# First convolution of a conv / deformable-conv kernel: its in-place chunk is computed ahead of the wait for copied rows, in the place of clock-starting matmuls of zeros

## The chip, the cores and the metric

The kernel runs on one core of one Trainium2 chip. The metric is the device time of one execution in microseconds (us). The engines are PE (TensorE, the matmul array), DVE (VectorE), ACT (ScalarE), POOL (GpSimd) and SP (SyncE, which only issues transfers here). PEld is the loading of PE's weights.

## The reference, cut to what matters

Two blocks work on `x` of shape (4, 32, 64, 64). The change touches the 3x3 convolution at the head of the first.

```python
def _L0_conv_ref(x, ...):        # x is the group-normalized input: one channel a group
    fa = _bn(_conv(x, conv_a_w, conv_a_b, pad=1), ...)      # 16 channels
    fb = _bn(_conv(x, conv_b_w, conv_b_b, pad=1), ...)      # 16 channels
    gh, gw, pr = _position_info(B, H, W, fa.dtype)
    att_a = _bn(_conv(concat([fa, gh, gw]), att_a_w, att_a_b), ...)     # 1x1, to one channel
    map_a = sigmoid(_conv(concat([att_a, gh, gw, pr]), attn_a_w, pad=1))
    ...                                                     # the same for b
    return concat([fa * (map_a * scale1), fb * (map_b * scale2)])

x = x + _L0_conv_ref(_gn(x), ...)
x = x + _L1_conv_ref(_gn(x), ...)    # modulated deformable 3x3 convolution, batch norm, relu
```

So the first convolution is: 4 images, 32 channels in, 32 out (both branches together), 64 x 64 pixels, 9 taps, all in float32.

## The kernel before

A program is written out by hand for each engine, and each engine runs its own instructions in the order in which they stand. Semaphores tie the engines together; a wait holds everything behind it on its engine.

**Where the data is.** The 128 partitions hold 4 images of 32 channels. `x_sb` is the input, `xpad` the normalized input with a border of zeros (image row y is row y + PAD_T). DVE and ACT each write `xpad` in two pieces: NORM1 gives DVE the image rows 0 to 16 and 17 to 33, ACT the rows 34 to 48 and 49 to 63. Each piece adds one to `norm1[0]` (DVE) or `norm1[1]` (ACT); `normalized(pe, norm1, NORM1, rows)` waits until the pieces up to that row are there.

**The first convolution** is done in two steps `s`, each of half the image: SPREAD = 4 chunks `k` of CH_ROWS = 8 rows (512 pixels), one PSUM bank a chunk. A tap of a step is 16 matmuls of 32 x 32 weights over 512 pixels, one for each chunk `k` and image `b`. The matmul of image `b` and chunk `k` takes its rows from the partitions of group (b + k) % 4 and writes those of group b, so that the 16 lie on the 16 different 32 x 32 tiles of the array. For k = 0 the two groups are the same, and the rows are read in place, from `xpad`: these are the 4 tiles of the diagonal. For k = 1, 2, 3 the rows have to stand on other partitions. `turn_rows` copies them there by transfers, six from SP and six from ACT (three a step on each), into `turned[0]` (in the memory of `hy`) and `turned[1]` (in that of `offs`); they count up `turned_in[0]` and `turned_in[1]`. The bank of a chunk gathers the 9 taps of all four images.

**The order on PE** around the change: a wait for the weights; a wait for DVE's first piece of `xpad`; `start_clock(20)`, 20 matmuls of the first padding rows of `xpad`, which are zeros, into the last bank; the waits for the normalized rows and for the copies of step 0; the 9 taps of step 0, after which `conv_ready` lets DVE and ACT move the four banks to `f_sb` (in the memory of `preg`, lines L1262 and L959); the waits for step 1; its taps 0 to 3; `att_step(0)`, 12 matmuls of 128 x 32 weights (L631), which need the moved banks of step 0; the taps 4 to 8 of step 1; then the attention maps of the chunks (`map_chunk`, L642), between which DVE, ACT and POOL put the block's output together and take the statistics of the second block.

Each float32 matmul has two records in the trace, so a tap of 16 matmuls shows as 32. Behind this stage come the offsets of the deformable convolution (L707, also 16 matmuls of 32 x 32 weights over 512 pixels a tap) and its long sampling loop (L844, from about 105 us to 310 us).

Of the kernel before, what the change touches and what calls it, by code (L numbers as in the profile page):

```python
# [7 lines left out]
B, C, H, W = 4, 32, 64, 64  # L8
NPIX = H * W
KK = 9  # L10
BR = C // 2
P128 = B * C
PAD_T = 2
XR, XC = H + 6, W + 2
AR = H + 2
CH_ROWS = 8
# [17 lines left out]
SPREAD = 4  # L34
# [19 lines left out]
BANK = 512  # L54
# [8 lines left out]
def conv_deform_kernel(nc, d, scratch, out):  # L63
# [8 lines left out]
    with ctx:  # L72
        def sb(name, shape, dt=f32):
            return ctx.enter_context(nc.sbuf_tensor(name, shape, dt))

        def sem(name):
            return ctx.enter_context(nc.semaphore(name))
# [3 lines left out]
        xpad = sb("xpad", [P128, XR, XC])  # L81
# [82 lines left out]
        ps = ctx.enter_context(nc.psum_tensor("ps", [P128, 8 * BANK], f32))  # L164
# [27 lines left out]
        norm1 = [sem(f"norm1_{n}") for n in ("vector", "scalar")]  # L192
# [4 lines left out]
        conv_ready = sem("conv_ready")  # L197
# [155 lines left out]
        NORM1 = ((0, 17), (17, 34)), ((34, 49), (49, H))  # L353
# [8 lines left out]
        def made_rows(i):  # L362

            return 2 * (i // B) + ZLEAD + i % B // 2, i % 2 * ZH
# [17 lines left out]
        def normalized(eng, done, pieces, rows):  # L382

            for n, sem_ in enumerate(done):
                needed = sum(pair[n][0] < rows for pair in pieces)
                if needed:
                    eng.wait_ge(sem_, needed)
# [215 lines left out]
        def _(pe):  # L603

            pe.wait_ge(w0_loaded, 16 * SPREAD)

            def conv_taps(s, taps):

                for t in taps:
                    dy, dx = t // 3, t % 3  # L610
                    for k in range(SPREAD):
                        for b in range(B):
                            g = slice((b + k) % SPREAD * C, ((b + k) % SPREAD + 1) * C)
                            if k == 0:
                                r = SPREAD * s * CH_ROWS + PAD_T - 1 + dy
                                rows = xpad[g, r:r + CH_ROWS, dx:dx + W]
                            else:
                                rows = turned[s][g, k, dy:dy + CH_ROWS, dx:dx + W]
                            at = (SPREAD * s + k) * BANK
                            mm = pe.matmul(ps[b * C:(b + 1) * C, at:at + BANK], w0[g, t, :], rows,  # L620
                                           start=t == 0, stop=t == KK - 1,
                                           tile_position=((b + k) % SPREAD * C, b * C))
                return mm
# [19 lines left out]
                          attrep[:, c * CH_ROWS + 1:(c + 1) * CH_ROWS + 1, 0:W],  # L643
                          start=True, stop=True).then_inc(map_ready, 1)

            def start_clock(n):


                for _ in range(n):
                    pe.matmul(ps[0:XC, 7 * BANK:7 * BANK + PAD_T * XC], xpad[:, 0, :], xpad[:, 0:PAD_T, :],  # L650
                              start=True, stop=True)

            pe.wait_ge(norm1[0], 1)
            start_clock(20)
            normalized(pe, norm1, NORM1, SPREAD * CH_ROWS + 1)
            pe.wait_ge(turned_in[0], 16 * len(TURNS))
            conv_taps(0, range(KK)).then_inc(conv_ready, 1)
            normalized(pe, norm1, NORM1, H)
            pe.wait_ge(turned_in[1], 16 * len(TURNS))
            conv_taps(1, range(0, 4))  # L660
            pe.wait_ge(attw_ready, 1)
            pe.wait_ge(fpad_zeroed, 2)
            att_step(0)
            conv_taps(1, range(4, KK)).then_inc(conv_ready, 1)
            pe.wait_ge(mapw_ready, 1)
            pe.wait_ge(pos_loaded, 16 * 2)
# [3 lines left out]
            for c in range(2, NCH):  # L670
# [6 lines left out]
                      start=True, stop=True).then_inc(codes_made, 1)  # L677
# [127 lines left out]
            for i in range(NT // 2):  # L805
# [20 lines left out]
                if 0 <= m < len(FAR_BLOCKS):  # L826
# [4 lines left out]
                              start=True, stop=True).then_inc(first_zmade, 1)  # L831

                if i < MAKERS:
                    n, at = made_rows(i)
# [13 lines left out]
                for turn in range(2):  # L848
# [5 lines left out]
                    elif turn == 1 and i == REACH_TURN + 1:  # L854
                        pe.wait_ge(reach_col, 1)
                        pe.matmul(ps[:, REACH_AT:REACH_AT + P128], later_far[:, :], identf[:, :],
                                  start=True, stop=True)
                    elif turn == 1 and i == REACH_TURN + 2:
                        pe.wait_ge(next_col, 1)
                        pe.matmul(ps[0:1, REACH_AT:REACH_AT + P128], reach_c[:, 1:2], identf[:, :],  # L860
                                  start=True, stop=True)
# [59 lines left out]
        def _(act):  # L921
# [21 lines left out]
            for _, (r0, r1) in NORM1:  # L943
                act.activation(inner[:, r0:r1, :], x3[:, r0:r1, :], ACT.Identity, bias=col(NSH), scale=col(RSTD))\
                    .then_inc(norm1[1], 1)
# [42 lines left out]
            for _, (r0, r1) in NORM2:  # L988
                act.activation(inner[:, r0:r1, :], x3[:, r0:r1, :], ACT.Identity, bias=col(NSH2), scale=col(RSTD2))\
                    .then_inc(norm2[1], 1)  # L990
# [663 lines left out]
```

## Time and profile before

| | |
|---|---|
| median of 3 runs | 334.06 us |
| lowest and highest of them | 333.67 and 336.54 us |
| the profiled execution's own time | 335.25 us |
| its span in the profile | 333.5 us |
| busy over the span | PE 79%, PEld 55%, DVE 81%, ACT 72%, POOL 63% |
| time from 0 to the first taps of the first convolution | 21.3 us |

The time is measured over the whole execution; the span runs from the first to the last profiled instruction. A busy share is an average over stages that differ: in the first 20 us DVE takes statistics and normalizes, from 21 us to 43 us PE computes the first convolution, and the sampling loop fills most of the rest. Times within the profile are counted from the start of the span.

### The profile page before, as it was taken

To read this page: it belongs to the slowest core of one execution; us is meant where nothing else is said; L and a number is where in the kernel's file an instruction comes from. 1 tells how busy PE (TensorE), PEld (TensorE's weight loads), DVE (VectorE), ACT (ScalarE), POOL (GpSimd) and SP (SyncE) were. 2 spreads that over 40 slices of the span, in tenths; PEclk is the share of its full clock that TensorE was granted. 3 is DMA by queue.
4 is the path that set the end of the run, shared out by engine and by line. 5 is a ranking of instruction groups with operands and counts; after the bars stand their busy time and mean duration, and the time that the engine had idled before them with its cause. 6 is when DMAs were issued, how large, how long until landed. Compare 5 with 4: busy or idle time off the path is not lost. (4 is left out here: it accounts for less than half of the span.)

```text
span 333.5 us, 16311 instructions
## 1 busy us (share of the span) xinstructions
PE 264.8 (79%) x7285; PEld 182.7 (55%) x7286; DVE 271.6 (81%) x513; ACT 238.8 (72%) x352; POOL 209.8 (63%) x162
## 2 busy tenths in 40 slices
PE   0399996988957887887899999998989998898340
PEld 0377422432416565656667676667656666776340
DVE  4743378824586999999999999998989999999676
ACT  1321355553865999888799999999989998997016
POOL 9200034400424878898789989998888999898300
PEclk9999997999997999999999999999999999999775
DMA  7891000000240120220000012000000200000006
GB/s 266 159 212 29 2 3 0 15 11 2 50 62 20 37 59 20 93 65 4 4 5 4 4 39 110 4 5 5 4 4 4 110 37 7 3 4 5 4 0 252
DMA packets 11956, 14.35 MB, mean 43 GB/s; under 512 B 4269, under 2 KB 7918, under 8 KB 11848
## 3 DMA queue, kind: packets, MB, share of 16 engines
q1 hardware_dynamic: 9852, 11.34, 11.7%
q10 hardware_dynamic: 1952, 1.34, 2.2%
q8 instruction: 58, 0.95, 1.3%
q0 software_dynamic: 80, 0.61, 0.9%
q14 instruction: 14, 0.11, 0.1%
HBM read 4.73 MB, written 2.98 MB: 23 GB/s over the span
## 5 line engine op out<-in xcount | busy, mean ns | idle before, releaser
L1439 DVE TENSOR_TENSOR prod<-ps,hy 128x480 f32<-128x480 f32 (+1 forms) x256 | 137.9, 600 | 7.6 <-PE ps L844 1.4
L844 PE MATMUL ps<-zreg,hx 64*64 64x96 f32 x4608 | 124.9, 248 | 19.6 <-DVE prod L1439 15.2
L585 POOL TENSOR_TENSOR prod<-prod 128x832 f32<-128x832 f32 x64 | 128.7, 2010 | 17.3 <-DVE prod L1439 15.0
L844 PEld LDWEIGHTS ps<-zreg,hx 64*64 64x64 f32 x4608 | 109.8, 133 | 38.6 <-ACT hx L1104 25.0
L995 ACT ACTIVATE hx<-ps 128x576 f32<-128x576 f32 x129 | 76.9, 648 | 19.2 <-PE ps L725 15.3
L1104 ACT ACTIVATE hx<-hx,rbias 128x1152 f32<-128x1152 f32 x63 | 79.8, 1267 | 0.4
L589 POOL TENSOR_TENSOR prod<-prod 128x320 f32<-128x320 f32 x64 | 50.7, 792 | 5.0
L1447 DVE TENSOR_REDUCE areg<-prod 128x64 f32<-128x576 f32 x64 | 48.3, 755 | 2.6 <-POOL prod L589 0.6
L725 PE MATMUL ps<-wz,xpad 32*64 32x144 f32 (+1 forms) x1024 | 35.1, 322 | 2.9 <-issue 1.3
L1099 ACT ACTIVATE zreg<-ps 128x576 f32<-128x576 f32 x56 | 37.0, 660 | 0.0
L561 POOL TENSOR_TENSOR x_sb<-prod,x_sb 128x512 f32<-128x512 f32 x8 | 10.1, 1268 | 42.4 <-DVE prod L1279 42.1
L693 PE MATMUL ps<-preg,sel 26*128 26x288 bf16 x256 | 26.9, 285 | 7.8 <-DMA preg<-scratch 4.1
L725 PEld LDWEIGHTS ps<-wz,xpad 32*64 32x64 f32 x1024 | 15.5, 130 | 23.3 <-issue 18.0
L707 PE MATMUL ps<-xpad,hx 32*32 32x512 f32 x576 | 20.9, 598 | 0.7 <-DVE zreg L1342 0.6
L620 PE MATMUL ps<-xpad,wreg 32*32 32x512 f32 x144 | 18.5, 595 | 0.4 <-DMA hy<-xpad 0.4
L937 ACT ACTIVATE small<-small 128x1 f32<-128x1 f32 (+1 forms) x5 | 1.0, 203 | 24.4 <-DVE small L1174 19.2
L650 PE MATMUL ps<-xpad 128*66 128x132 f32 x40 | 7.4, 370 | 13.6 <-DVE xpad L1217 13.6
L570 POOL CAST prod<-wreg 128x512 bf16<-128x512 f32 x4 | 3.7, 915 | 22.0 <-DVE wreg L1327 22.0
L1342 DVE COPY zreg<-ps 128x1152 f32<-128x1152 f32 x4 | 5.4, 1358 | 14.4 <-PE ps L725 14.4
L693 PEld LDWEIGHTS ps<-preg,sel 26*128 26x128 bf16 x256 | 7.8, 92 | 17.2 <-issue 5.6
L650 PEld LDWEIGHTS ps<-xpad 128*66 128x66 f32 x40 | 7.2, 201 | 13.2 <-issue 13.2
L707 PEld LDWEIGHTS ps<-xpad,hx 32*32 32x32 f32 x576 | 7.4, 103 | 9.8 <-issue 8.4
(158 smaller groups left out, 265.9 us busy)
## 6 DMA issues: line engine op xcount, KB each, us to landing
zreg<-zreg SPq DMA_DIRECT2D x12, 288.0 KB, 2.4
out<-x_sb SPq DMA_DIRECT2D x7, 256.0 KB, 2.1
x_sb<-in_x SPq DMA_DIRECT2D x3, 512.0 KB, 5.0
preg<-scratch SPq DMA_DIRECT2D x12, 54.0 KB
zreg<-in_pos POOLq DMA_DIRECT2D x1, 528.0 KB, 5.2
x_sb<-in_x SPq DMA_DIRECT2D x2, 256.0 KB, 6.5
scratch<-parts SPq DMA_DIRECT2D x12, 36.0 KB
scratch<-prod SPq DMA_DIRECT2D x10, 36.0 KB
```

Of the source, the lines that this page charges most:

```text
L585: pool.tensor_tensor(slots[:, :, 0:2 * moved], slots[:, :, 0:2 * moved], slots[:, :, 2 * KEPT:6 * KK], ALU.add).then_inc(half_folded, 1)
L589: pool.tensor_tensor(slots[:, :, 0:2 * moved], slots[:, :, 0:2 * moved], slots[:, :, 2 * SUMMED:2 * KEPT], ALU.add).then_inc(folded, 1)
L620: mm = pe.matmul(ps[b * C:(b + 1) * C, at:at + BANK], w0[g, t, :], rows, start=t == 0, stop=t == KK - 1, tile_position=((b + k) % SPREAD * ...
L693: mm = pe.matmul(dist_ps(PAIR_BANKS[u])[:, h, :], sel[u * C:u * C + SELK, b, :], px[u][:, :, y // 2 * W + h * HALF:y // 2 * W + (h + 1) * ...
L707: mm = pe.matmul(ps[j * C:(j + 1) * C, at:at + BANK], woff[b * C:(b + 1) * C, t, :], xpad[b * C:(b + 1) * C, r:r + CH_ROWS, dx:dx + W], st ...
L725: mm = pe.matmul(ps[g * W:(g + 1) * W, b * BANK + at:b * BANK + at + c1 - c0], xpad[b * C:(b + 1) * C, n + g * HH, 1:1 + W], wz[b * C:(b + ...
L844: return pe.matmul(g_ps(g, h)[u * W:(u + 1) * W, k - TAPS[h][0], :, :], hx[s, (t + u) % 4, k, :], z_sb[s, b, at:at + 3, k * C:(k + 1) * C] ...
L995: act.activation(hx[:, t % 4, :, :].rearrange("p k (h x) -> p h k x", h=2), dist_ps(bank).rearrange("p h (k x) -> p h k x", k=KK), ACT.Abs)\
L1099: act.activation(z_sb[:, :, n % ZRING, at:at + ZH], zt_ps(KK * HALF, ZH), ACT.Copy)\
L1104: act.activation(dist[:, slot:slot + 2, :], dist[:, slot:slot + 2, :], ACT.Relu, bias=rbias[:, 0:1], scale=-1.0).then_inc(hx_ready, 2)
L1439: mul = vector.tensor_tensor(pv[:, n0:n1], gv, wv[:, n0:n1], ALU.mult)
L1447: vector.tensor_reduce(here, prod[:, i % 2 * 2:i % 2 * 2 + 2, :] .rearrange("p g (a n e) -> p g a e n", a=C // 2, e=2)[:, :, :, :, 0:SUMME ...
```

## The change

`conv_taps` gets an argument `shifts`, the chunks `k` that it computes. The function `start_clock` and its 20 matmuls of zeros go. In their place, behind the same wait for DVE's first piece, stand the in-place chunk (k = 0) of all 9 taps of step 0 and, behind the wait for all normalized rows, that of the taps 0 to 3 of step 1: 13 x 4 = 52 matmuls. The other three chunks of the same taps, 13 x 12 = 156 matmuls, come behind the waits for the copies. The taps 4 to 8 of step 1 keep all four chunks together. The number of useful matmuls is the same.

```diff
-            def conv_taps(s, taps):
+            def conv_taps(s, taps, shifts=range(SPREAD)):
...
-                    for k in range(SPREAD):
+                    for k in shifts:
...
-            def start_clock(n):
-
-
-                for _ in range(n):
-                    pe.matmul(ps[0:XC, 7 * BANK:7 * BANK + PAD_T * XC], xpad[:, 0, :], xpad[:, 0:PAD_T, :],
-                              start=True, stop=True)
-
             pe.wait_ge(norm1[0], 1)
-            start_clock(20)
-            normalized(pe, norm1, NORM1, SPREAD * CH_ROWS + 1)
+            in_place, copied = range(1), range(1, SPREAD)
+            conv_taps(0, range(KK), in_place)
+            normalized(pe, norm1, NORM1, H)
+            conv_taps(1, range(4), in_place)
             pe.wait_ge(turned_in[0], 16 * len(TURNS))
-            conv_taps(0, range(KK)).then_inc(conv_ready, 1)
-            normalized(pe, norm1, NORM1, H)
+            conv_taps(0, range(KK), copied).then_inc(conv_ready, 1)
             pe.wait_ge(turned_in[1], 16 * len(TURNS))
-            conv_taps(1, range(0, 4))
+            conv_taps(1, range(4), copied)
```

Only PE's program changes. In the rows below, `ps<-xpad,wreg` is a matmul of an in-place chunk (`wreg` holds the weights), `ps<-hy,wreg` one of a copied chunk of step 0, `ps<-offs,wreg` one of step 1; x4 and x12 are numbers of matmuls. PE's program from its first wait, before:

```order
L650 MATMUL ps<-xpad 66x132 [waits norm1_vector,w0_loaded]
L650 MATMUL ps<-xpad 66x132 x19
L620 MATMUL ps<-xpad,wreg 32x512 [waits turned_in0,norm1_scalar,norm1_vector]
L620 MATMUL ps<-xpad,wreg 32x512 x3
L620 MATMUL ps<-hy,wreg 32x512 x12
```

The same place of the changed kernel:

```order
L620 MATMUL ps<-xpad,wreg 32x512 [waits norm1_vector,w0_loaded]
L620 MATMUL ps<-xpad,wreg 32x512 x35
L620 MATMUL ps<-xpad,wreg 32x512 [waits norm1_scalar,norm1_vector]
L620 MATMUL ps<-xpad,wreg 32x512 x15
L620 MATMUL ps<-hy,wreg 32x512 [waits turned_in0]
L620 MATMUL ps<-hy,wreg 32x512 x107
```

The 20 matmuls of zeros are gone, 52 matmuls of the diagonal tiles stand ahead of the wait for `turned_in0`, and behind it come groups of 12 without the 4. Next, PE from the end of step 0 to the attention step, before (the lines left out are three more pairs of x4 and x12):

```order
L620 MATMUL ps<-hy,wreg 32x512 x12
L620 MATMUL ps<-xpad,wreg 32x512 [waits turned_in1,norm1_scalar,norm1_vector]
L620 MATMUL ps<-xpad,wreg 32x512 x3
L620 MATMUL ps<-offs,wreg 32x512 x12
...
L631 MATMUL ps<-preg,attw 32x512 [waits f_ready,fpad_zeroed,attw_ready]
L631 MATMUL ps<-preg,attw 32x512 x11
```

The same place of the changed kernel:

```order
L620 MATMUL ps<-hy,wreg 32x512 x107
L620 MATMUL ps<-offs,wreg 32x512 [waits turned_in1]
L620 MATMUL ps<-offs,wreg 32x512 x47
L631 MATMUL ps<-preg,attw 32x512 [waits f_ready,fpad_zeroed,attw_ready]
L631 MATMUL ps<-preg,attw 32x512 x11
L620 MATMUL ps<-xpad,wreg 32x512 x4
```

Between the end of step 0 and the attention step there were 4 taps of 16 matmuls, and there are now 4 of 12.

## Rows read from the trace of the kernel before

**Rows 1.** Timeline of PE, 8 to 50 us: start, length, what, count.

```profile
13.56 7.38 PE L650 MATMUL ps<-xpad 128*66 128x132 f32 x40 [13.56 <-DVE xpad L1217]
21.32 0.63 PE L620 MATMUL ps<-xpad,wreg 32*32 32x512 f32 x4 [0.38 <-DMA hy<-xpad]
...
30.55 0.63 PE L620 MATMUL ps<-xpad,wreg 32*32 32x512 f32 x4
...
35.43 2.78 PE L631 MATMUL ps<-preg,attw 128*32 128x512 f32 x24
38.14 0.63 PE L620 MATMUL ps<-xpad,wreg 32*32 32x512 f32 x4
...
43.59 1.98 PE L642 MATMUL ps<-zreg,wreg 128*128 128x512 f32 x4
```

**Rows 2.** Waits of PE from 0 to 70 us: total, times, longest.

```profile
PE ps L650 <- DVE xpad L1217: 13.6, 1, 13.6
PE ps L642 <- DVE prod L1279: 2.2, 2, 1.9
PE ps L642 <- DVE zreg L1271: 1.2, 1, 1.2
...
PE ps L620 <- DMA hy<-xpad: 0.4, 1, 0.4
```

**Rows 3.** Timeline of ACT and DVE from 0 to 40 us.

```profile
31.61 1.45 ACT L959 ACTIVATE preg<-ps,small 128x512 f32<-128x512 f32 x2 [8.17 <-PE ps L620]
31.64 1.53 DVE L1262 TENSOR_SCALAR preg<-ps,small 128x512 f32<-128x512 f32 x2 [5.36 <-PE ps L620]
```

**Rows 4.** Windows with L650 alone: stretch, length, busy (records) of PE and PEld, granted clock.

```profile
16.50:17.50 1.00, 1.00 (x6) 1.00 (x5) 1.00 1.12 203
17.50:18.50 1.00, 1.00 (x7) 1.00 (x6) 1.00 1.02 214
...
19.00:19.50 0.50, 0.50 (x6) 0.50 (x5) 1.00 1.06 238
19.50:20.00 0.50, 0.50 (x7) 0.50 (x6) 1.00 1.01 222
20.00:20.50 0.50, 0.50 (x7) 0.50 (x6) 1.00 1.04 275
```

**Rows 5.** Timeline of PEld in the attention step, 35.3 to 38.4 us.

```profile
35.43 0.16 PEld L631 LDWEIGHTS ps<-preg,attw 128*32 128x32 f32 x8 [0.84 <-issue]
35.88 0.13 PEld L631 LDWEIGHTS ps<-preg,attw 128*32 128x32 f32 x4 [0.30 <-issue]
36.31 0.13 PEld L631 LDWEIGHTS ps<-preg,attw 128*32 128x32 f32 x4 [0.30 <-issue]
36.74 0.13 PEld L631 LDWEIGHTS ps<-preg,attw 128*32 128x32 f32 x4 [0.30 <-issue]
```

**Rows 6.** Windows of all engines: PE, PEld, DVE, ACT, POOL, granted clock, DMA share, GB/s.

```profile
24.00:25.00 1.00, 1.00 (x52) 0.69 (x34) 0.86 (x5) 0.00 (x0) 0.00 (x0) 1.00 1.03 122
25.00:26.00 1.00, 1.00 (x50) 0.71 (x34) 0.86 (x5) 0.00 (x0) 0.00 (x0) 1.00 0.35 66
26.00:27.00 1.00, 1.00 (x42) 0.63 (x18) 0.28 (x1) 0.00 (x0) 0.00 (x0) 1.00 0.09 21
...
54.00:55.00 1.00, 1.00 (x2) 0.25 (x2) 0.86 (x3) 0.00 (x0) 1.00 (x2) 0.50 0.00 0
```

**Rows 7.** Timeline of PE, 66 to 106 us: taps of L707, transposes of L718.

```profile
82.34 3.40 PE L707 MATMUL ps<-xpad,hx 32*32 32x512 f32 x96 [0.60 <-DVE zreg L1342]
85.67 1.53 PE L718 MATMUL ps<-identf,areg 128*128 128x128 f32 x12
87.83 0.66 PE L718 MATMUL ps<-identf,areg 128*128 128x128 f32 x4 [0.64 <-ACT areg L1024]
...
101.02 3.60 PE L718 MATMUL ps<-identf,wreg 128*128 128x128 f32 x16
```

## The prediction

> **What bounds the kernel now.** I read the order of work on PE first (its timeline), then PE's waits, then what DVE and ACT wait for. PE does nothing of use until DVE has normalized its first piece: 13.6 us [rows 2]. From 13.56 to 20.94 it runs the 20 matmuls of zeros (40 records), waits 0.38 us for the copied rows, and starts the taps at 21.32 [rows 1]. From there to the maps at 43.59 PE has no wait at all: the next ones are those of L642 [rows 2]. DVE and ACT on the other hand wait for PE there, 5.36 and 8.17 us until step 0 is complete [rows 3]. So between 21.3 and 43.6 us PE is the bound, and every microsecond by which its taps end later is handed to DVE, ACT and POOL, which work on the taps' output. Before 21.3 us the bound is the transfer of the copies, and PE has 7.8 us (13.56 to 21.32) in which it could do something useful. The change fills them. The question is whether what it puts there shortens what comes after by as much as it takes.
>
> **What a tap costs.** The nine taps of step 0 run from 21.32 to 30.55 [rows 1]: 9.23 / 9 = 1.03 us for 16 matmuls, side by side on 16 tiles. From 30.55 to 35.43 there are 4 taps: 4 x 1.03 = 4.10, and 0.78 is left over, which I read as the draining of the last matmuls before the array goes over to weights of 128 rows. Then the attention step, 35.43 to 38.14 [rows 1]: 12 matmuls on 4 tiles, three rounds of 4. Its weights are loaded in groups of 4 at 35.88, 36.31 and 36.74 [rows 5], one each 0.43 us, two records a matmul, so one round of 4 matmuls takes 0.86 us. This is the row on which the forecast rests. A round of 4 costs nearly as much as one of 16 (0.86 against 1.03), because each tile must stream its 512 pixels through, however many tiles run beside it. Splitting a tap of 16 into one of 4 and one of 12 therefore saves very little of the second part, and pays the first almost in full.
>
> **The terms.**
> (a) Removed: 20 matmuls of zeros, 7.38 us, and the 0.38 us wait. Both lay under the transfer, so their removal gives nothing by itself; what counts is that PE is free from 13.56 on.
> (b) The clock. One effect of the matmuls of zeros is to be kept in the sum: up to 18.5 us 6 to 7 of their records fall in a microsecond, and from 19.5 us 7 in half a microsecond [rows 4]. [...] Before the change only zeros were slowed. Now useful matmuls stand there. I take 19.25 as the moment.
> (c) The in-place taps, 9 + 4 = 13 rounds of 4 matmuls. [...] From 13.56 to 19.25, 5.69 / 1.72 = 3.31 rounds; the other 9.69 x 0.86 = 8.33 us. End: 27.58. The upper bound for a round is 1.03, the price of one of 16, which would add 13 x 0.17 = 2.2 us.
> (d) The wait for the copies of step 0 costs nothing: they were in by 21.3 [rows 1], 6.3 us before PE asks. The copies of step 1 are asked for later still; the transfers fade between 25 and 27 us [rows 6]. The wait for all normalized rows stands nine rounds in, past 23 us, when DVE and ACT have long gone on.
> (e) The copied taps, 13 rounds of 12. Not in the trace. Bounds: 0.86 (a round of 4) and 1.03 (of 16); 12 lies between, and I take the middle, 0.95. 13 x 0.95 = 12.35, end 39.93; with the bounds 38.8 and 41.0.
> (f) The drain before the attention step, 0.78, as before: 40.71.
> (g) The attention step waits for the moved banks of step 0. Before, DVE had them at 31.64 + 1.53 = 33.17 [rows 3], 2.3 us ahead of 35.43. Now the copied taps of step 0 end about 27.58 + 8.55 = 36.13, one tap of drain and hand-over later (before: 31.64 - 30.55 = 1.09) the moving starts, at 37.2, and ends at 38.75, 2.0 us ahead of 40.71. Still covered, because the cover shrinks from 4 taps of 16 to 4 of 12, by 0.3 us only.
> Sum: the attention step starts at 40.71 instead of 35.43, **5.3 us later**. Nothing behind it changes in order or work, the five last taps of step 1 included, and no engine has other work with which to catch up, so I carry the 5.3 us to the end. The profiled execution (335.25 us, of which 333.5 are span) would become 340.5; against the median of the runs, 334.06, I forecast 339.3.
>
> What can move that: the moment of (b). If the clock were up at once the sum would be 2.85 us less, if it rose 2 us later, 1.0 more. And the later stretches at half clock, such as 54 to 55 us [rows 6], may fall on other work after a shift: 16 records of the transposes at 101 us took 3.60 us, where 12 and 4 at 85.67 and 87.83 took 1.53 + 0.66 = 2.19 [rows 7]. That is 1.4 us either way. With these and the bounds of (e) the forecast's own range is 336.5 to 342.5; the 2.2 us of (c) can take its end to 343.
>
> [...] All four in-place matmuls of a tap write one bank, from four different groups of rows. In the trace the same happens in each of the four banks, and 16 matmuls still go through in 1.03 us; in the second convolution (L707) each group of rows has a bank to itself, and three taps of 16 take 85.67 - 82.34 = 3.33 us, 1.11 a tap [rows 1, 7]. So sharing a bank costs nothing visible.
>
> [...]
>
> **The rivals.**
> 1. Faster: the records decide, not the streaming. If PE were bound by the number of matmuls that it issues, 1.03 us for 16 would be 0.26 for 4 and 0.77 for 12. The 13 in-place rounds would take 13 x 0.52 = 6.8 us even at half clock and be done at 20.3, ahead of the copies; the copied taps would take 21.32 + 13 x 0.77 + 0.78 = 32.1, 3.3 us earlier than 35.43: 330.8. For it speaks that 16 matmuls take longer than 4 (1.03 against 0.86); against it the attention step, where 4 take 0.86 and not 0.26. The point at which it decides: with p for a round of 4 and q for one of 12, PE is at the attention step at 13.56 + 2.85 + 13 (p + q) + 0.78, and that is 35.43 for p + q = 1.40. The forecast has 1.81, and two rounds can't be under 1.72 as long as 0.86 holds for each. Chance of a gain or of no loss by this: 0.07.
> 2. The clock stays down. The in-place rounds use 4 tiles of 16, and no row shows such a thin round for longer than the attention step's 2.7 us. If it does not count as work enough, all 13 rounds take 1.72: 13.56 + 22.4 = 35.9; if the clock then rises at once, the attention step starts at 35.9 + 12.35 + 0.78 = 49.1, 13.6 us late, and if it takes the 5.7 us that it took before, about 2.9 more: 347.7 to 350.6. Against it: PE would be busy without a gap, and the attention step and the zeros keep or raise the clock. Chance 0.09.
> [...] Chance 0.01.
> 4. Little changes: the clock comes up near 14 us, rounds of 12 cost 0.86, and a stretch at half clock falls away further on: 5.3 - 2.85 - 1.2 - 1.4, about 0. Or the later stages hide some of the delay after all. Chance 0.08.
>
> [...]
>
> **How the numbers follow.** The forecast has 0.75, the rivals 0.07, 0.09, 0.01 and 0.08. One per cent, about what a measurement can tell from no change here, is 3.3 us: 330.7 to 337.4. Faster than that: half of rival 1, 0.04. Within it: the rest of rival 1, rival 4 and the lowest part of the forecast's range (0.04), 0.15. Slower: 0.81. The range runs from 336.4 to 343.0: it holds nearly all of the forecast and a part of rival 4, and leaves out rivals 1 to 3.
>
> **What would show it.** In the timeline of PE: in-place records from 13.6 us at a pace of 1.7 us a round, then of 0.86 from about 19; the first `hy` record at 27.6 with no wait before it (right), or at 21.3 after a wait (rival 1), or after 35 (rival 2, with the clock column or the pace at half). Rounds of 12 between 0.86 and 1.03 us. The attention step near 40.7, without a wait. The same number of us behind it as before. I am wrong if a round of 4 on the diagonal is much cheaper than one in the attention step, if the clock behaves otherwise under thin rounds, or if a later stage absorbs the delay.

## Result and the profile after

The changed kernel took 338.21 us (median of 4 runs, 337.80 to 340.98), the kernel before 334.57 (4 runs). The ratio is 1.0109, 95% interval 1.0071 to 1.0148. A second comparison on one chip (e8 below, 10 runs against 29) gave 1.0056, 1.0030 to 1.0082. Both intervals lie above 1. By the medians the change costs 3.6 us in the first comparison and 2.6 in the second, and the second ratio alone would be 1.9 us; the two profiled executions lie 3.0 us apart (338.29 and 335.25). It is slower, by 0.6 to 1.1%.

The timeline of PE after the change, from the first in-place round to the maps, answers to [rows 1]:

```profile
13.83 12.40 PE L620 MATMUL ps<-xpad,wreg 32*32 32x512 f32 x92 [13.83 <-DVE xpad L1211]
25.66 0.80 PE L620 MATMUL ps<-hy,wreg 32*32 32x512 f32 x8
26.05 0.61 PE L620 MATMUL ps<-xpad,wreg 32*32 32x512 f32 x4
26.12 0.77 PE L620 MATMUL ps<-hy,wreg 32*32 32x512 f32 x9
26.48 0.61 PE L620 MATMUL ps<-xpad,wreg 32*32 32x512 f32 x4
26.66 0.66 PE L620 MATMUL ps<-hy,wreg 32*32 32x512 f32 x4
26.91 0.61 PE L620 MATMUL ps<-xpad,wreg 32*32 32x512 f32 x4
27.09 7.50 PE L620 MATMUL ps<-hy,wreg 32*32 32x512 f32 x186
...
38.37 2.78 PE L631 MATMUL ps<-preg,attw 128*32 128x512 f32 x24
41.09 0.63 PE L620 MATMUL ps<-xpad,wreg 32*32 32x512 f32 x4
...
46.53 1.99 PE L642 MATMUL ps<-zreg,wreg 128*128 128x512 f32 x4
```

The in-place rounds start at 13.83, and PE has no wait until the maps: the 0.38 us for the copies are gone, and the next waits of PE are those of L642, as before. But the attention step (L631) starts at 38.37 instead of 35.43, 2.94 us later, and the maps (L642) at 46.53 instead of 43.59, the same 2.94 us. The first matmuls of the sampling loop follow 2.7 us later (108.78 against 106.09), and the span ends 3.0 us later (336.5 against 333.5). So the delay of this stage is the delay of the whole kernel.

How long a round of 4 takes is best read from its weight loads, one group of 4 for each of a round's two records (timeline of PEld):

```profile
16.36 0.23 PEld L620 LDWEIGHTS ps<-xpad,wreg 32*32 32x32 f32 x4 [0.63 <-issue]
17.21 0.22 PEld L620 LDWEIGHTS ps<-xpad,wreg 32*32 32x32 f32 x4 [0.63 <-issue]
18.07 0.22 PEld L620 LDWEIGHTS ps<-xpad,wreg 32*32 32x32 f32 x4 [0.63 <-issue]
18.75 0.13 PEld L620 LDWEIGHTS ps<-xpad,wreg 32*32 32x32 f32 x4 [0.46 <-issue]
19.18 0.13 PEld L620 LDWEIGHTS ps<-xpad,wreg 32*32 32x32 f32 x4 [0.30 <-issue]
19.61 0.13 PEld L620 LDWEIGHTS ps<-xpad,wreg 32*32 32x32 f32 x4 [0.30 <-issue]
```

Up to 18.07 a group comes each 0.85 us, 1.71 a round; from 18.75 each 0.43, 0.86 a round. The pace doubles near 18.6, under rounds that use 4 tiles of 16, and I read it as the clock going from half to full. The clock column says 1.00 from 13 us on, as in [rows 4], and up to 18.6 the pace contradicts it; e7 below has a stretch where the column itself says 0.50 and the weight loads come at half their rate. The second half, the rounds of 12, in windows (engines as in [rows 6]):

```profile
19.00:27.00 8.00, 8.00 (x101) 2.83 (x97) 5.17 (x27) 1.89 (x4) 0.00 (x0) 1.00 0.86 178
27.00:38.00 11.00, 11.00 (x303) 7.88 (x287) 1.53 (x2) 1.45 (x2) 0.00 (x0) 1.00 0.05 14
```

287 weight loads in 11.0 us are 26.1 in a microsecond; a round of 12 has 24, so it takes about 0.9 us, start and end of the stretch included (e6 below shows nine of them in 7.72 us, 0.86 each). DVE takes over step 0 at 35.16, and not at 31.64 as before (second row of [rows 3]):

```profile
35.16 1.53 DVE L1256 TENSOR_SCALAR preg<-ps,small 128x512 f32<-128x512 f32 x2 [8.29 <-PE ps L620]
```

It is done at 36.69, 1.7 us ahead of the attention step, which still does not wait for it.

### The profile page after: what moved, and what is told of

Read it like the earlier page. It is cut to its first block and busy times, and to the rows that moved or that the text cites. A ratio compares the mean times of both kernels' runs of the same rounds, so it can differ in the third digit from the quotient of the medians.

```text
span 336.5 us, 16230 instructions
## 1 busy us (share of the span) xinstructions
PE 265.9 (79%) x7245; PEld 176.8 (53%) x7246; DVE 271.5 (81%) x513; ACT 238.7 (71%) x352; POOL 209.8 (62%) x162
## 5 line engine op out<-in xcount | busy, mean ns | idle before, releaser
L838 PE MATMUL ps<-zreg,hx 64*64 64x96 f32 x4608 | 121.8, 247 | 19.1 <-DVE prod L1433 12.8
L838 PEld LDWEIGHTS ps<-zreg,hx 64*64 64x64 f32 x4608 | 107.9, 132 | 36.9 <-ACT hx L1098 24.3
L701 PE MATMUL ps<-xpad,hx 32*32 32x512 f32 x576 | 20.9, 598 | 0.7 <-DVE zreg L1336 0.6
L620 PEld LDWEIGHTS ps<-xpad,wreg 32*32 32x32 f32 x144 | 6.0, 115 | 24.6 <-issue 23.5
L642 PE MATMUL ps<-zreg,wreg 128*128 128x512 f32 x16 | 9.9, 727 | 3.6 <-DVE prod L1273 2.2
```

What stands on the lines that cost most here:

```text
L701: mm = pe.matmul(ps[j * C:(j + 1) * C, at:at + BANK], woff[b * C:(b + 1) * C, t, :], xpad[b * C:(b + 1) * C, r:r + CH_ROWS, dx:dx + W], st ...
L838: return pe.matmul(g_ps(g, h)[u * W:(u + 1) * W, k - TAPS[h][0], :, :], hx[s, (t + u) % 4, k, :], z_sb[s, b, at:at + 3, k * C:(k + 1) * C] ...
```

## Experiments

Line numbers shift by some lines between the kernels; the names are the same. "Start of the attention step" is the first record of `ps<-preg,attw`, 35.43 in the kernel before and 38.37 after the change.

**e1: in place only the nine rounds of step 0.**

```diff
-            normalized(pe, norm1, NORM1, H)
-            conv_taps(1, range(4), in_place)
+            normalized(pe, norm1, NORM1, SPREAD * CH_ROWS + 1)
             pe.wait_ge(turned_in[0], 16 * len(TURNS))
             conv_taps(0, range(KK), copied).then_inc(conv_ready, 1)
+            normalized(pe, norm1, NORM1, H)
             pe.wait_ge(turned_in[1], 16 * len(TURNS))
-            conv_taps(1, range(4), copied)
+            conv_taps(1, range(0, 4))
```

> In place and early are only the nine rounds of step 0; the taps 0 to 3 of step 1 are whole again (16 matmuls). Theory F (streaming floor): a round of 4 and a round of 12 each cost 0.86 us, a whole tap 1.03 to 1.07, so each split tap costs 0.7 us more than a whole one, and only what lies before 21.3 us is free. Nine rounds, the first 4.7 us of them at half clock, end near 23.9; the attention step should start at 35.6 to 35.8, against 38.37 after the change and 35.43 before it: 0.2 to 0.4 us slower than before, no change that can be measured. Theory C (the loss of the change is only useful work done at half clock): the same cold rounds stand here, so the loss should stay near 3 us. Theory W (the loss is the later hand-over of step 0 to DVE and ACT): the hand-over is still later than before by under 1 us, so the loss is that.

Measured: ratio to before 1.0009 (0.9983 to 1.0036), medians 336.10 and 335.15, no change. Its profile:

```profile
13.35 8.12 PE L620 MATMUL ps<-xpad,wreg 32*32 32x512 f32 x60 [13.35 <-DVE xpad L1211]
21.01 0.69 PE L620 MATMUL ps<-hy,wreg 32*32 32x512 f32 x8
...
34.27 2.78 PE L631 MATMUL ps<-preg,attw 128*32 128x512 f32 x24
```

The loss of the change is gone with the four rounds of step 1, though the first rounds are still at half clock. That speaks against theory C, less strongly than planned: by the weight loads (0.86 us apart up to 15.89, 0.43 from 16.57) the clock was up by 16.4 in this execution, 3.0 us after the first round. For that reason, and with a start at 13.35, the attention step comes even 1.2 us earlier than before, which I had not worked out (35.6 to 35.8); the span (334.2 against 333.5) and the 10 runs show no gain from that. What becomes of such a gain is taken up under e6.

**e2: in place only six rounds.** As e1, with `conv_taps(0, range(6), in_place)`, then `conv_taps(0, range(6), copied)` and `conv_taps(0, range(6, KK))`.

> In place and early are six rounds of step 0, as many as I work out to end at 21.3 us, when the copies are there; taps 6 to 8 and all of step 1 are whole. Theory F: no round lies beyond the free time, and six groups of 12 cost 0.86 instead of 1.03: the attention step starts at 34.4, 1.0 us earlier than before; the ratio to before is 0.997, a gain at the limit of what can be measured. Theory C: the rounds at half clock are under the transfer and cost nothing, no change. If splitting a tap has a price of its own (a drain between the parts), 0 to 1 us slower.

Measured: 0.9980 (0.9957 to 1.0003), medians 334.83 and 335.15. The sign is that of theory F (0.997), but the interval holds 1 as well, which is theory C here, so this run does not decide between them. The profile of this kernel was taken at a mean clock of 0.749, and its times are not read. A loss of more than 0.1 us, the upper end of the interval, is excluded.

**e3: the matmuls of zeros taken away, nothing in their place.**

```diff
             pe.wait_ge(norm1[0], 1)
-            start_clock(20)
             normalized(pe, norm1, NORM1, SPREAD * CH_ROWS + 1)
```

> The kernel before without its 20 matmuls of zeros, nothing put in their place. It measures what the zeros are worth. If the clock starts to rise only when PE starts its taps at 21.3 us, about 5 us of whole taps run at half clock, 1.71 instead of 1.03 us each: 2 us slower than before (1.3 to 2.8). If the clock were up without them, no change.

Measured: 1.0054 (1.0023 to 1.0086), 1.7 us by the medians (336.81 and 335.15). The windows of its profile:

```profile
23.00:25.00 2.00, 2.00 (x50) 1.01 (x35) 1.72 (x9) 0.63 (x2) 0.00 (x0) 1.00 0.79 123
25.00:27.00 2.00, 2.00 (x50) 1.14 (x36) 1.29 (x6) 0.00 (x0) 0.00 (x0) 1.00 0.34 85
27.00:29.00 2.00, 2.00 (x81) 1.42 (x64) 0.00 (x0) 0.00 (x0) 0.00 (x0) 1.00 0.10 23
29.00:31.00 2.00, 2.00 (x85) 1.75 (x68) 0.00 (x0) 0.00 (x0) 0.00 (x0) 1.00 0.00 0
```

35 or 36 weight loads in two microseconds up to 27, 64 to 68 behind: by this pace the first 6 us of whole taps ran at half clock (the column says 1.00 here too), and the attention step starts at 37.89, 2.46 us later than before. So the zeros were worth about 2 us (1.7 by the medians, 2.46 at the attention step), and the in-place rounds, under which the clock rises too (near 18.6 in the profile after the change), replace them in this.

**e4: the changed kernel with the clock raised early.** `start_clock` is defined and called ahead of everything on PE, where the border of `xpad` has just been zeroed (the definition is left out here).

```diff
+            pe.wait_ge(xpad_zeroed, 1)
+            start_clock(24)
             pe.wait_ge(w0_loaded, 16 * SPREAD)
```

> The changed kernel with 24 matmuls of zeros put ahead of all, from the moment the border of the normalized input is zeroed (4.8 us), so that the clock is up when the first useful round starts at 13.8 us. Theory F: 13 rounds at 0.86 end at 25.0, 2.3 us earlier than after the change; the attention step starts at 36.0, still 0.6 us later than before: 2.3 us faster than the changed kernel, 0.6 slower than before. Theory C: the whole loss of 2.9 us goes. If the clock falls again between the zeros and 13.8 us, nothing is gained.

Measured: 0.9982 (0.9954 to 1.0010) to before, medians 335.15 and 335.15: the loss is gone. The changed kernel was not run beside it; set against e8, on another chip, the two ratios to before lie 0.0074 apart, 2.5 us.

```profile
4.79 8.16 PE L609 MATMUL ps<-xpad 128*66 128x132 f32 x48 [4.79 <-POOL xpad L547]
13.48 10.08 PE L629 MATMUL ps<-xpad,wreg 32*32 32x512 f32 x92 [0.53 <-DVE xpad L1220]
22.97 0.80 PE L629 MATMUL ps<-hy,wreg 32*32 32x512 f32 x8
...
35.67 2.78 PE L640 MATMUL ps<-preg,attw 128*32 128x512 f32 x24
```

The attention step starts 2.7 us earlier than after the change and 0.24 later than before; F had 36.0. The clock is up for the useful rounds: 11 records of the zeros fall in the two microseconds up to 10, 19 in the two behind, and the weight loads of the in-place rounds come 0.43 us apart from 13.91 on. By time alone C fits as well here (all but 0.24 of its 2.9 us are gone). e1 and e5 decide between the two.

**e5: the zeros kept where they were, and the in-place rounds behind them.** Now almost nothing of the 13 rounds is hidden and all of them run at full clock. The definition of `start_clock` is kept too and left out here.

```diff
             pe.wait_ge(norm1[0], 1)
+            start_clock(20)
             in_place, copied = range(1), range(1, SPREAD)
             conv_taps(0, range(KK), in_place)
```

> The changed kernel with the 20 matmuls of zeros kept ahead of the in-place rounds, so that these start near 20.9 us, at full clock, and no part of them is hidden by the transfer. It measures the price of splitting 13 taps. Theory F (streaming floor, 0.86 for a round of 4 and of 12): 13 x (0.86 + 0.86) less the 0.9 us by which the two groups overlap where they meet; the attention step starts at 43.1, 7.7 us later than before. If the number of matmuls issued decided, splitting would be free: 13 x 1.03 and the start 0.4 us earlier, no change against before.

Measured: 1.0167 (1.0132 to 1.0203), 341.68 against 335.60 (4 and 29 runs).

```profile
13.64 6.50 PE L650 MATMUL ps<-xpad 128*66 128x132 f32 x40 [13.64 <-DVE xpad L1219]
20.07 10.07 PE L620 MATMUL ps<-xpad,wreg 32*32 32x512 f32 x92
29.56 0.81 PE L620 MATMUL ps<-hy,wreg 32*32 32x512 f32 x8
29.97 0.60 PE L620 MATMUL ps<-xpad,wreg 32*32 32x512 f32 x4
...
42.29 2.78 PE L631 MATMUL ps<-preg,attw 128*32 128x512 f32 x24
```

From the first in-place record to the attention step 22.22 us pass, where 13 whole taps took 14.11 (21.32 to 35.43). Worked out, 13 x 1.72 + 0.78 less an overlap of 0.9 is 22.24. There is no half clock in this stretch (the weight loads come 0.43 us apart from 20.52 on), so theory C cannot explain it, and a bound by the number of matmuls would give 14. The split costs 8.1 us for 13 taps. The attention step comes 6.86 us later than before, and not 7.7, because the rounds start at 20.07 here and not at 20.9: 1.25 us before the whole taps did. The changed kernel sets the 7.5 us from 13.83 to 21.3 against the 8.1, but the first 4.8 of them count half, because of the clock: 8.1 - 7.5 + 2.4 = 3.0, where 2.94 were measured.

**e6: the early zeros of e4 and the nine rounds of e1.** Only as many rounds as fit before the copies.

> The zeros early (24, from 4.8 us), and in place and early only the nine rounds of step 0, which at full clock just fit before the copies: 13.6 + 9 x 0.86 = 21.3. Theory F: nine groups of 12 at 0.86, then nine whole taps: the attention step starts at 34.0, 1.4 us earlier than before, ratio to before 0.996. What comes behind may take from it what the place of the half-clock stretch near 100 us costs (it was 3.4 us long before the change and 10.2 us in two experiments, where the transposes and the first samples took about 1 us more): so 333.2 to 334.6 against 334.6 of before.

Measured: 0.9955 (0.9926 to 0.9985), 334.49 against 335.60 (12 and 29 runs): faster than the kernel before, and 3.7 us faster than the changed one beside it (338.16).

```profile
13.44 7.93 PE L629 MATMUL ps<-xpad,wreg 32*32 32x512 f32 x72 [0.41 <-DVE xpad L1220]
21.58 7.93 PE L629 MATMUL ps<-hy,wreg 32*32 32x512 f32 x209 [0.20 <-DMA hy<-xpad]
...
29.30 0.59 PE L629 MATMUL ps<-offs,wreg 32*32 32x512 f32 x1
...
33.95 2.78 PE L640 MATMUL ps<-preg,attw 128*32 128x512 f32 x24
```

The rounds end 0.20 us before the copies land, which is the fit aimed at. The nine copied rounds run from 21.58 to 29.30, 0.86 each. The attention step starts 1.48 us earlier than before (34.0 expected). The medians keep 1.1 us of it. In the profile 0.86 is left at 100 us (99.81 against 100.67), and nothing at the first sample. That part is lost near 100 us, where PE waits about 4 us for a transfer (4.10 before, 4.00 in e6) and the clock falls to 0.50. Windows there, first before, then e6:

```profile
100.00:105.00 5.00, 3.94 (x20) 3.38 (x20) 2.45 (x5) 2.52 (x4) 2.42 (x4) 0.66 0.15 29
105.00:110.00 5.00, 4.01 (x141) 2.94 (x145) 4.93 (x9) 3.62 (x6) 1.62 (x2) 1.00 0.05 10
```

```profile
100.00:105.00 5.00, 4.30 (x24) 3.40 (x20) 2.72 (x5) 2.52 (x4) 1.71 (x4) 0.50 0.15 30
105.00:110.00 5.00, 5.00 (x113) 3.60 (x109) 4.38 (x8) 2.88 (x4) 1.63 (x2) 0.58 0.09 17
```

The clock is at 1.00 again from 105 us before, and only in the later part of the second window in e6. From the first record of L693 at 100.67 to the first sample at 106.09 it took 5.42 us before, in e6 6.27 (99.81 to 106.08). e1, e4, e5 and e7 show the same 6.27, the changed kernel 5.39. The half clock lasts on into e6's loop, whose end comes 0.65 us later than before (first record of the transposes behind it 314.25 against 313.60); that the span is still 0.2 shorter (333.3) is due to these transposes, 5.23 us against 6.54. So this profile shows the gain of the first stage, and not how the runs keep 1.1 us of it. Whether the loss near 100 us happens in each run no experiment here shows.

**e7: the kernel before with the 24 early matmuls of zeros added to its 20.**

> The kernel before with the 24 early matmuls of zeros added and its 20 kept. PE's taps still start when the copies are there, at full clock as before: no change, 0.9985 to 1.0015. If it is faster, the gain of the early-clock experiments has another source than the in-place rounds.

Measured: 1.0020 (0.9989 to 1.0050), no gain. So the early zeros bring nothing without the rounds that stand before the copies. This is no test of the early clock alone: the taps did not start at full clock, as expected. In the profile the 20 kept zeros, at full clock (40 records in 4.69 us, before in 7.38), end at 18.6 instead of 20.9, PE waits 2.17 us for the copies, and the clock is down from about 21 on (the column has 0.54 from 21 to 22 and 0.50 from 22 to 24, with 33 weight loads there against 65 before), so that the attention step starts at 36.22, 0.79 us later than before:

```profile
20.81 0.87 PE L629 MATMUL ps<-xpad,wreg 32*32 32x512 f32 x4 [2.17 <-DMA hy<-xpad]
```

```profile
22.00:24.00 2.00, 2.00 (x49) 0.86 (x33) 1.59 (x9) 1.58 (x3) 0.00 (x0) 0.50 1.12 224
```

**e8: the changed kernel again.**

> The changed kernel again, beside the others on one chip, since its first result rests on four runs: 3.0 us slower than before by the shift of the attention step, ratio 1.009 (1.007 to 1.011).

Measured: 1.0056 (1.0030 to 1.0082), medians 338.16 and 335.60; the ratio is below the 1.007 to 1.011 expected. The attention step starts at 38.37 again, the span is 336.9. The two parts differ: the rounds start at 13.30, 0.53 us earlier than in the first profile, and by the weight loads the clock rises near 19.1 and not 18.6. That the sum is the same to 0.01 us is chance.

**e9: the kernel of e6 with the tiles of a tap in another order.** `for b in range(B)` outside, `for k in shifts` inside.

> The kernel of e6 with the 16 matmuls of a tap in another order: images outside, chunks inside, so that four in a row go to one group of columns and four banks, where they went to four groups of columns and one bank. It asks why a whole tap takes 1.03 to 1.07 us where a round of 12 takes 0.86. If the order in which the tiles are fed is the reason, the whole taps of step 1 should come down, towards 0.86 (or go up). If it is only the number of matmul and weight-load records in a tap (64 against 48) that PE can look ahead over, the pace stays: four whole taps from the first record of step 1 to the attention step in 4.6 to 4.8 us, as in e6.

Measured in one run: 333.37 beside 335.38 for one run of the kernel before, too few to say that it differs from e6. The four whole taps from step 1's first copied record to the attention step take 4.66 us (29.42 to 34.08), in e6 4.65 (29.30 to 33.95). The order is not the reason for a whole tap's extra 0.2 us. Whether it is the number of records is taken up in the last section.

## Why the prediction was right

The forecast was 339.3 in a range of 336.4 to 343.0, slower with a chance of 0.81; the result was 338.21. The totals lie closer together than the losses, 5.3 and 3.6 us: 0.5 us of the nearness is luck, since the median of the kernel before, 334.06 when the forecast was made, became 334.57. Step by step, on the profiled execution, where I had the attention step at 40.71 and it came at 38.37:

- **What a tap costs** held. A round of 4 takes 0.86 us, and the 12 matmuls that are left of a tap take no less; e5 shows it with nothing else in the way (22.22 us for 13 of each, the overlap and the 0.78 in it), and it is why the change loses.
- **(b), the clock.** The 19.25 was my choice between the 19.0 and 19.5 of [rows 4]; it rose near 18.6, with a start 0.27 later; together with the round price the in-place rounds ended at 27.34 (26.91 and half a round) instead of 27.58: 0.24 us less.
- **(c)** No row gave the 1.72 by itself; it was twice the 0.86 of [rows 5], by the halved pace of [rows 4], and the weight loads after the change show 1.71. The 0.86 held: the diagonal tiles cost what the attention step's do.
- **(d)** held: no wait for either set of copies. The 0.78 of **(f)** was not measured by itself, and that it is a drain was my reading; what the profiles show is that the weight loads of L631 stand idle 0.84 us just before it, after the change as in [rows 5]. I keep the 0.78 below.
- **(e) was mis-sized.** I took 0.95 for a round of 12, between my bounds; it is at the lower one, 0.86. 13 x 0.09 = 1.17 us.
- **(e) also lacked an overlap.** I let the copied rounds start when the in-place ones end, 27.34. Their first records start at 25.66, and 27.34 + 13 x 0.86 + 0.78 = 39.30 is 0.93 more than measured. By 27.1 21 records of `hy` have started, of the 24 of the first copied round (x8, x9 and x4 in the timeline above): about one round ran beside the last in-place ones. The 0.93 is what the sum leaves, so an error in the drain would be in it. The sum of the three, 0.24 + 1.17 + 0.93, is the 2.34 us.
- **(g) and the rest** held: the banks were ready 1.7 us ahead (2.0 forecast); 2.94 us at the attention step, 2.94 at the maps, 3.0 at the end.
- **The range** was too narrow below. The forecast's own 336.5 takes off the 2.85 us of the clock alone; with the lower bound of (e), which the text says is in it and which is what came, it would be 335.3.

Of the rivals, 1 (the number of matmuls decides) fell with e5 for rounds of 4 and of 12, and 2 (the clock stays down) with the weight loads after 18.75. The chance of 0.01 went to a large cost of sharing a bank; the runs show none: four in-place records in one bank come each 0.43 us, 0.86 a round. Rival 4 held in one of its three parts, rounds of 12 at 0.86. The clock came at 18.6 and not near 14, and the half-clock stretch near 100 us did not fall away (5.39 us to the first sample against 5.42). The forecast's 5.3 us was half as much again as the first result (3.6) and twice the second (2.6 by the medians); the direction and the cause were right, the size too large by (e). As to the cause, the loss goes when the clock is up early (e4), and it goes as well when four fewer rounds stand early (e1). These are two ways of shortening one overrun. The 13 rounds end at 27.34, 6.02 us after the whole taps started before; what then stands before the attention step takes 11.03 us, and not 14.11, so only 3.08 of the 6.02 come back. The difference is the 2.94 us.

## What to carry to other kernels

Work put into a wait is free only as far as the wait reaches. The matmuls here run side by side on 32 x 32 tiles, and a batch of 16 split into 4 and 12 cost a full pass for each part (0.86 + 0.86 us against 1.03 to 1.07, e5). Where a split costs that, move only as many rounds forward as end when the wait does: 13 rounds made this kernel slower, 9 of them, or 13 with the clock raised beforehand, made no difference that could be measured, and 9 with the clock raised beforehand made it faster by 0.45% (0.15 to 0.74). The filler under which the clock rose was worth about 2 us of its own here (1.7 by the medians of e3, 2.46 at its attention step), and such a value is to be priced before it goes.

## What the runs showed of the hardware

The text ahead of the prediction says that each engine runs its instructions in the order in which they stand. The matmuls here did not start strictly in that order. All 52 in-place matmuls stand ahead of the first copied one, and yet 8 records of `hy` start at 25.66 and in-place ones at 26.05, 26.48 and 26.91. The same is in e1 (21.01), e4 (22.97) and e5 (29.56), each 1.6 to 1.7 us before the in-place rounds end, and the time agrees with it: 0.9 us less than end to end. The matmuls that start ahead of their turn lie on other tiles of the array than those they pass.

The clock rose under rounds on 4 tiles of 16 as it did under the zeros with their weights of 128 x 66: 4.8 us after the first in-place round here, 3.0 in e1, 5.8 in e8, and 5.4 to 5.9 after the first zeros before [rows 4]. The reading rests on the pace, while the column says 1.00. Where the column falls, in e7, pace and column agree: 33 weight loads of whole taps in the two microseconds at 0.50 (22 to 24), 67 in two at 1.00 (26 to 28).

A round of 12 costs no more than a round of 4 (0.86 us), a whole tap of 16 costs 1.03 to 1.07. The extra 0.2 us is there at full clock only. Starts of whole taps, first at full clock in the kernel before, then at half clock in e3:

```profile
23.25 0.83 PE L620 MATMUL ps<-xpad,wreg 32*32 32x512 f32 x4
24.32 0.80 PE L620 MATMUL ps<-xpad,wreg 32*32 32x512 f32 x4
```

```profile
22.97 1.35 PE L620 MATMUL ps<-xpad,wreg 32*32 32x512 f32 x4
24.68 1.56 PE L620 MATMUL ps<-xpad,wreg 32*32 32x512 f32 x4
26.39 1.42 PE L620 MATMUL ps<-xpad,wreg 32*32 32x512 f32 x4
```

At full clock they lie 1.07 us apart, at half clock 1.71, which is what a round of 4 takes at that clock too. So the last four tiles are free at half clock. A second bound that does not follow the clock would do this: a whole tap has 64 records (matmuls and weight loads), 1.07 us are 16.7 ns for each, and at that rate the 48 of a round of 12 would take 0.80 us, below the 0.86 measured. That is an estimate from these rows, and rival 1 in a small part; e9 excludes the order of the tiles, and no run here varies the number of records alone, so the cause stays open.
